# Split weights kept in device memory, and another slot schedule, in a fused four-layer float32 kernel

## The reference

```python
x = field_step(x)                                        # layer 0: stencils, once, at the start
# layer 1, for each of the 16 batch entries (S = D = 512, 16 heads of 32, F = 2048)
x = ln(src) * (1 + scale) + shift
q, k, v = x @ Wq + bq, x @ Wk + bk, x @ Wv + bv
probs = softmax(where(mask, -inf, q @ k.T / sqrt(32) + attention_bias))
x = x + (probs @ v) @ Wo + bo
h = ln(x) * g2 + beta2
x = x + gelu2(h @ W1 + b1) @ W2 + b2                     # gelu2(t) = t * sigmoid(1.702 t)
# layer 2
hidden = gelu(x @ down_W.T + down_b)                     # 512 -> 128
hidden = hidden @ expert_W[id].T + expert_b[id] + emb[id]
x = ln(hidden @ up_W.T + up_b + x) * gamma + beta
# layer 3: rotate each pair of columns
out[0::4], out[1::4] = x0*ct + x1*st, -x0*st + x1*ct     # and the same for pairs 2, 3 with phi
```

## Time and profile before

| what | value |
|---|---|
| median of three runs | 4944.82 us (4941.17 to 4945.67) |
| profiled execution, its own time | 4945.61 us |
| its span, first to last instruction | 4943.8 us |
| PE busy | 4197.9 us, 85% |
| DVE, ACT, POOL busy | 59%, 49%, 31% |
| mean granted PE clock | 0.935 of full speed |
| moved by DMA | 700.26 MB, 142 GB/s on average |

### The profile page before, as it was taken

How to read it: one execution, slowest core, us unless ns; L and a number is a source line. 1 busy time by engine, 2 the same in 40 slices (tenths; PEclk the granted TensorE clock), 3 DMA queues, 4 the chain that set the end, 5 groups by cost and what they waited for, 6 DMA issues and landing times.

```text
span 4943.8 us, 72563 instructions
## 1 busy us (share of the span) xinstructions
PE 4197.9 (85%) x25315; PEld 3075.7 (62%) x25720; DVE 2912.8 (59%) x6296; ACT 2416.5 (49%) x5064; POOL 1550.6 (31%) x1069
## 2 busy tenths in 40 slices
PE   6994789797988979797988979797978889797977
PEld 3442567575766757575766657575756667575755
DVE  8993455565555555565556555555656555555454
ACT  0002555455555555554555555455555555555542
POOL 0002124233333333233333333333333333333334
PEclk9997899899999989899999989899999989899988
DMA  3224555554545455554545455554545455554521
GB/s 118 103 95 143 168 156 163 143 153 128 162 138 164 132 154 154 143 160 125 163 133 170 135 150 152 147 165 125 161 133 164 135 148 152 151 163 126 146 88 58
DMA packets 530343, 700.26 MB, mean 142 GB/s; under 512 B 45232, under 2 KB 250848, under 8 KB 529984
## 3 DMA queue, kind: packets, MB, share of 16 engines
q1 hardware_dynamic: 521024, 677.76, 47.4%
q10 hardware_dynamic: 8448, 16.78, 0.9%
q0 software_dynamic: 512, 1.05, 0.1%
HBM read 527.20 MB, written 33.62 MB: 113 GB/s over the span
## 4 chain that ended last, share of the span: by engine, by line
PE 58%; DVE 12%; POOL 5%; ACT 4%; issue 4%; another core or an unknown queue 4%; DMA 4%; SPq 1%; POOLq 0%; ACTq 0%; DVEq 0%
PE bank L824 42%; PE bank L886 6%; PE bank L877 4%; PE bank L907 3%; DVE prob L1065 3%; POOL w L616 2%; PE bank L878 2%; POOL tok L658 1%; POOL tok L660 1%; DMA raw<-in_L_cond_W 1%; DVE zT L1114 1%; ACT probT L707 1%; DVE stats L511 1%; DMA stack<-parts 1%
## 5 line engine op out<-in xcount | busy, mean ns | idle before, releaser
L616 POOL TENSOR_TENSOR w<-raw,w 128x512 fp32r<-128x512 f32 x768 | 1031.8, 1348 | 2362.6 <-ACT w L691 2361.4
L707 ACT ACTIVATE probT<-bank 128x512 f32<-128x512 f32 x1024 | 609.8, 595 | 1569.4 <-PE bank L886 1565.5
L886 PE MATMUL bank<-ident,prob 128*128 128x128 f32 x4096 | 646.1, 282 | 303.6 <-ACT probT L707 281.7
L824 PE MATMUL bank<-zT,w 128*128 128x512 f32 x3072 | 828.1, 420 | 29.0 <-issue 28.1
L824 PE MATMUL bank<-w,gparts 128*128 128x512 f32 x3072 | 791.7, 406 | 13.2 <-DVE gparts L1120 13.2
L886 PEld LDWEIGHTS bank<-ident,prob 128*128 128x128 f32 x4096 | 520.7, 146 | 450.9 <-ACT prob L699 288.3
L699 ACT ACTIVATE prob<-prob,low 128x512 f32<-128x512 f32 x1024 | 732.5, 715 | 7.2 <-DVE low L1065 7.0
L824 PEld LDWEIGHTS bank<-zT,w 128*128 128x128 f32 x3072 | 597.1, 196 | 166.3 <-issue 36.9
L1065 DVE CUSTOM_DVE_ANT_0 prob<-bank,prob 128x512 f32<-128x512 f32 x1024 | 697.8, 681 | 0.3 <-issue 0.3
L824 PEld LDWEIGHTS bank<-w,gparts 128*128 128x128 f32 x3072 | 578.7, 189 | 133.8 <-POOL w L616 11.1
L877 PE MATMUL bank<-stack 128*128 128x512 f32 x1024 | 517.7, 506 | 165.7 <-DVE low L1065 148.3
(11 more groups left out here) (175 smaller groups left out, 5197.6 us busy)
## 6 DMA issues: line engine op xcount, KB each, us to landing
prob<-in_fside_Bx16xSxS SPq DMA_DIRECT2D x512, 512.0 KB, 3.8
stack<-parts SPq DMA_DIRECT2D x1024, 128.0 KB, 3.1
raw<-in_L_cond_W SPq DMA_DIRECT2D x512, 256.0 KB, 2.7
field<-in_x SPq DMA_DIRECT2D x16, 1024.0 KB, 5.4
x<-total ACTq DMA_DIRECT2D x16, 1024.0 KB, 5.9
xin<-x SPq DMA_DIRECT2D x16, 1024.0 KB, 6.8
raw<-in_L_cond_Wq SPq DMA_DIRECT2D x64, 256.0 KB, 3.0
raw<-in_L_cond_Wk SPq DMA_DIRECT2D x64, 256.0 KB, 4.4
```

What stands on the lines that cost most here:

```text
L616: pool.tensor_tensor(w[m % RING][:, 1, :], raw[m % RAWS][:], w[m % RING][:, 0, :].bitcast(F32), ALU.subtract).then_inc(w_lo, 1)
L707: act.activation(probT[:, m % TURNED, :], turned[:], ACT.Copy).then_inc(turn_copied, 1)
L824: mm = te.matmul(dst, stat(hs, k), mov(hm, k), start=start and n == 0, stop=stop and n == count - 1)
L886: mm = te.transpose(turned[:, k * P:(k + 1) * P], prob[:, m % PROBS, k * P:(k + 1) * P], ident[:])
```

## The change

**Weights are split once.** Only the 48 units of batch entry 0 (`FRESH`) go through `raw`, ACT and POOL. SP then stores both halves, 512 KB, to a scratch tensor `split_w` (`store_split`), and every later use is one 512 KB load from there straight into the ring (`load_split`): SP waits until PE has released the buffer and issues the load; PE waits for `w_in`. `SPLIT_AT` allows at most one fresh unit in a slot.

**ACT's order in a slot** is now `copy_turned(t)` and then `exp(t + 2)`.

**The slots move.** Feed forward, Y, layers 2 and 3, Q, K and V come 1 to 6 slots earlier. The turn of the next input goes from slot 49, where all four column blocks were turned through the `sums` banks, to slots 36 to 39, one block a slot through the bank `turned`, with the high part on ACT ahead of `copy_turned`, the rest on DVE behind its feed-forward work, and PE waiting for the latter before `turn_block`. Up and V blocks alternate in slots 50 to 56 (`UP_AT`, `UP_BANK`, `V_BANK`). `scale_context` comes one slot earlier.

**Work changes engine.** `number_mask` goes to POOL. The sine products of the rotation go to POOL (four 128 x 512 `tensor_scalar`, behind beta), and DVE is left with two `scalar_tensor_tensor` over 1024 elements. The copy into `fence` in `score_step` is gone.

```diff
-QK_AT = ((51, 52), (0, 1), (14, 15), (31, 33))
-CTX_SCALE_AT, CTX_LAST_AT, O_AT = 2, 3, 5
-Z_TURN_AT = 10
-FF_AT = 13
-STATS_AT, ADAPT_AT, LOAD_X_AT, EXPERT_AT = 18, 26, 11, 20
-Y_AT, X_TURN_AT, Y_TURN_AT = 47, 49, 51
-DOWN_AT, EXPERT_MM_AT, UP_AT = 53, 54, 55
-V_AT = (53, 54, 57, 58)
-NORM_AT, ROTATE_AT = 57, 63
-MASK_AT = (59, 60, 61, 62)
-CTX_AT = 60
-V_BANK = (1, 2, 0, 1)
+QK_AT = ((45, 47), (0, 2), (16, 18), (30, 32))
+CTX_LAST_AT, O_AT, Z_TURN_AT = 1, 3, 8
+FF1_AT, FF2_AT = 11, 14
+LOAD_X_AT, STATS_AT, ADAPT_AT, EXPERT_AT, X_TURN_AT = 8, 18, 26, 20, 36
+Y_AT, Y_TURN_AT, DOWN_AT, EXPERT_MM_AT = 44, 46, 48, 50
+V_AT, UP_AT = (50, 52, 54, 56), (51, 51, 53, 53)
+V_BANK, UP_BANK = (1, 2, 3, 2), (3, 0, 1, 0)
+NORM_AT, ROTATE_AT = 55, 62
+MASK_AT = (49, 53, 57, 61)
+CTX_AT = 57
 def ff1_slot(f):
-    return FF_AT if f == 0 else FF_AT + 2 + 2 * f - 1
+    return FF1_AT + 2 * f
 def ff2_slot(f):
-    return FF_AT + 2 + 2 * f + 2 if f < NF - 1 else Y_AT
+    return FF2_AT + 2 * f
...
+                def store_split(slot):
+                    for m in FRESH:
+                        if SPLIT_AT[m] == slot:
+                            i = ORDER[m]
+                            sp.wait_ge(w_lo, i + 1)
+                            sp.dma_start(split_w[i], w[m % RING][:].rearrange("p h n -> p (h n)").bitcast(F32)).then_inc(w_stored[m % RING], 16)
+                            if i + RAWS < len(FRESH):
+                                load_raw(sp, FRESH[i + RAWS])
+                def load_split(slot):
+                    for m in range(RING, len(UNITS)):
+                        if UNITS[m - RING][2] == slot and m not in ORDER:
+                            await_release(sp, m - RING)
+                            kind, _, k = UNITS[m][0]
+                            i = KINDS[kind, k]
+                            sp.wait_ge(w_stored[FRESH[i] % RING], 16 * same_place(FRESH[i], True))
+                            sp.dma_start(w[m % RING][:].rearrange("p h n -> p (h n)").bitcast(F32), split_w[i]).then_inc(w_in[m % RING], 16)
...
+                        if c < B and X_TURN_AT <= s < X_TURN_AT + KB:
+                            x_hi_part(c, s - X_TURN_AT)
+                        if t < BLOCKS:
+                            copy_turned(t)
                         if t + EXP_LEAD < BLOCKS:
                             exp(t + EXP_LEAD)
-                        if t < BLOCKS:
-                            copy_turned(t)
...
                 def unit(kind, b, k):
                     m = UNIT[kind, b, k]
-                    te.wait_ge(w_lo, m + 1)
+                    if m in ORDER:
+                        te.wait_ge(w_lo, ORDER[m] + 1)
+                    else:
+                        te.wait_ge(w_in[m % RING], 16 * same_place(m, False))
                     return w[m % RING]
...
                         if t < BLOCKS:
+                            if c < B and X_TURN_AT <= s < X_TURN_AT + KB:
+                                te.wait_ge(x_lo, KB * c + s - X_TURN_AT + 1)
                             turn_block(t)
...
-                    v.tensor_copy(fence[:, m % 7:m % 7 + 1], scal[:, 0, 0:1])
...
+                                for h in range(2):
+                                    sine = scal[:, a, 4 + 2 * h:5 + 2 * h]
+                                    pool.tensor_scalar(crossed[:, :, 2 * h], quads[:, :, 2 * h + 1], sine, None, ALU.mult).then_inc(sined, 1)
+                                    pool.tensor_scalar(crossed[:, :, 2 * h + 1], quads[:, :, 2 * h], sine, -1.0, ALU.mult, ALU.mult).then_inc(sined, 1)
```

More of the change, by code:

```diff
@@ L86, in weight_units, with split_slots, same_place @@
             t = SLOTS * n + s
[L87 to L88 removed]
+            if n and s == O_AT:
+                units += [(("o", n - 1, k), t, t + TB - 1) for k in range(KB)]
             for f in range(NF if n else 0):
                 if s == ff1_slot(f):
[L91 removed]
+                    units.append((("w1", n - 1, f), t, t))
                 if s == ff2_slot(f):
[L93 removed]
+                    units.append((("w2", n - 1, f), t, t))
             for g in range(1, G) if n < B else ():
                 if s in QK_AT[g]:
[L96 removed]
+                    units.append((("qk"[QK_AT[g].index(s)], n, g), t, t))
             if n + 1 < B:
                 if s in QK_AT[0]:
[L99 to L101 removed]
+                    units.append((("qk"[QK_AT[0].index(s)], n + 1, 0), t, t))
+                if s == V_AT[0]:
+                    units += [(("v", n + 1, k), t, SLOTS * n + V_AT[-1]) for k in range(KB)]
     return units
 UNITS = weight_units()
[L106 to L111 removed]
+UNIT = {name: m for m, (name, _, _) in enumerate(UNITS)}
+FRESH = [m for m, (name, _, _) in enumerate(UNITS) if name[1] == 0]
+ORDER = {m: i for i, m in enumerate(FRESH)}
+KINDS = {(kind, k): i for i, (kind, _, k) in enumerate(UNITS[m][0] for m in FRESH)}
+def split_slots():
+    slots = {}
+    last = -3
+    for m in FRESH:
+        if m >= RING:
+            last = max(last, UNITS[m - RING][2]) + 1
+            assert last < UNITS[m][1] + 2, (UNITS[m], last)
+        slots[m] = last
+    return slots
+SPLIT_AT = split_slots()
+def same_place(m, fresh):
+    return sum(1 for u in range(m % RING, m + 1, RING) if (u in ORDER) == fresh)
 class Link:
@@ L535, in early_statistics @@
         def early_statistics(link, v):
-            for q in range(TB):
-                number_mask(v, 0, q)
             v.wait_ge(x_in, 16)
@@ L574, in _ @@
                     load_bias(sp, pair)
-                next_units(-3)
-                next_units(-1)
+                store_split(-3)
                 for j in range(HG):
                     load_stack(0, j)
+                for slot in (-2, -1):
+                    store_split(slot)
+                    load_split(slot)
                 for n in range(B + 1):
@@ L627, in _ @@
                 split_lo(-3)
-                split_lo(-1)
+                for q in range(TB):
+                    number_mask(pool, 0, q)
                 pool.wait_ge(consts_in, 16 * 12)
@@ L631, in _ @@
                 pool.tensor_tensor(xin[0][:], xin[0][:], bcast(row["bo"]), ALU.add).then_inc(xin_biased, 1)
-                split_lo(0)
+                for slot in (-2, -1):
+                    split_lo(slot)
                 for n in range(B + 1):
@@ L748, in _ @@
                     q_hi(0, 0, c)
-                split_hi(-1)
                 for q in range(TB):
@@ L753, in _ @@
                     exp(m)
-                split_hi(0)
+                for slot in (-2, -1):
+                    split_hi(slot)
                 for n in range(B + 1):
@@ L801, in _ @@
                         if c < B:
-                            if s == X_TURN_AT:
-                                for k in range(KB):
-                                    x_hi_part(c, k)
                             if s in QK_AT[0]:
@@ L980, in _ @@
                                 for k in (2 * (s - Z_TURN_AT), 2 * (s - Z_TURN_AT) + 1):
-                                    turn(tok, k, z_turned)
+                                    turn(sums[k], tok, k, z_turned)
                             for f in range(NF):
@@ L1224, in _ @@
                             tail(a, s)
-                        if c < B and s in MASK_AT:
-                            number_mask(v, c, s - MASK_AT[0])
                         if n < B and CTX_AT < s < CTX_AT + G:
```

205 lines of the change are left out of this document (99 added, 106 removed).

## The result

Four runs of the changed kernel have a median of 4900.24 us (4880.8 to 4902.56), four of the kernel before 4945.24 us (4941.17 to 4950.87). The ratio is 0.990, with a 95% interval of 0.9872 to 0.9927. So the change gains 45 us, where 235 were forecast, and the time is above the range (4590 to 4860). The profiled execution took 4898.9 us, with a span of 4897.1.

What follows compares the result with a forecast made beforehand. PE bounds slots 14 to 45; elsewhere it waits for splits, mask and DVE. A middle n: 8.1 - 5.7 - 21.0 + 2.5 = -16.1 us; all n 235, so 4945.6 becomes 4711 us, range 4590 to 4860.

Steps and rivals of the forecast that it cites:

- 10.3 us wait: Old slots 60 and 61: PE waits for `copy_turned` behind weight split and DVE mask; forecast to have no cause left.
- 4.8 and 1.9 us waits: Old slots 10 to 13: waits for a weight split and for DVE's `z_lo`; forecast gone, window gain 5.7 us.
- this is covered: Feed forward: exponential delays `tanh` and `g_hi` by 0.91 us each, against about 1.3 us to spare.
- the starving feed forward: What would make the forecast most wrong: ACT's new order starves the feed forward, and all 16 column blocks pay.
- Four O loads in slot 56: 2 MB ahead of bias and stack loads, with a clock drop after the `ctx_lo` wait: may take 2.5 us per entry.
- n = 0 and n = 1: a gain of 6 and of 5: First two entries: n = 0 gains 6 us (mask, fewer splits), n = 1 gains 5 despite 512 KB stores beside 36 splits.
- hidden, unless POOL needs over 1.7: Four sine products on POOL at 1.2 us each, done 14 us after the normed rows; DVE needs them some 16 after.
- The 2 us for `g_lo` behind POOL: Slot 39: POOL's addition to xin (4.5 us) starts there and holds DVE's `g_lo`, another 2 us.
- B: Rival: DMA becomes the bound in the feed forward, a middle n gets 14 us longer, 5100 us; chance 0.07.
- A: Rival: POOL's gamma, beta and slow sine products hold `ctx_lo` and rotation, PE waits some 10 us; 4828 us; chance 0.15.
- C: Rival: PE's clock stays up without the long waits, 8 us more gained per middle n, 4607 us; chance 0.12.
- D: Rival: no help; the long wait is really the chain through beta, something as long replaces it; about 4940 us; chance 0.03.

Runs made afterwards that it cites:

- e6: Changed kernel with exponential first, `scale_context` one slot later, output bias added in slot 52, O loads spread over slots 61, 62, 63 and 0: 4720.09 us, 0.9566.
- e13: e6 with the rotation's second half done in slot 63, not directly behind the first in slot 62: 4685.69 us, 0.9477.
- e4: Changed kernel with ACT doing `exp(t + 2)` ahead of `copy_turned(t)` again, as before the change: 4835.56 us, 0.9786.
- e9: Kernel before, with only ACT's new order (`copy_turned` ahead of the exponential): 4980.51 us, 1.0074.
- e1: Changed kernel with each O unit reload cut to 64 KB of its 512 KB, leaving out part of the computation: 4837.27 us, 0.9776.
- e10: Changed kernel with the four O loads in full, issued one each in slots 61, 62, 63 and 0, not together in slot 56: 4839.14 us, 0.9795.
- e11: Changed kernel with every one of the 720 stored-weight reloads cut to 64 KB, stores unchanged, leaving out part of the computation: 4816.43 us, 0.9743.
- e2: Changed kernel with `scale_context` back by one slot, from slots 17, 33 and 49 to 18, 34 and 50: 4854.59 us, 0.9816.
- e12: e11 with the stores of split blocks cut to 64 KB too: 4804.64 us, 0.972.
- e7: Changed kernel with exponential first, `scale_context` one slot later, output bias added in slot 52, gamma and beta in quarters; O loads still in slot 56: 4799.17 us, 0.9717.
- e14: e13 with a second operation (times 1.0) in the two sine products that had one: 4665.81 us, 0.9418.
- e8: e6 with gamma and beta in quarters and a second operation (times 1.0) in the plain sine products: 4710.02 us, 0.9521.

## Why the prediction was wrong

Per entry, by its own stretches (e6 is the changed kernel with four delays taken out, e13 with five):

| slots | predicted | changed kernel | e6 | e13 |
|---|---|---|---|---|
| 3 to 11 | 36.3 | 36.2 | 35.0 | 35.3 |
| 12 to 42 | 143.8 | 149.7 | 143.3 | 142.8 |
| 43 to 2 | 80.4 | 86.3 | 81.3 | 78.0 |
| all | 260.5 | 272.2 | 259.6 | 256.2 |

The main mechanism was right: with the splits gone the 10.3 us wait of the earlier trace rows and the 4.8 and 1.9 us waits of the earlier trace rows are gone, and the longest wait of PE in n = 2 to 14 is 5.1 us. That slots 3 to 11 came out to 0.1 us is in part luck: the terms given for them add up to 36.1, not 36.3, and 1.1 us of what was measured is the delay of `z_hi` in slot 11 that no term held (e4). The likeliest case was priced for a schedule without collisions, and four of its steps failed.

- *"this is covered"* (the exponential ahead of `tanh` and `g_hi`). It holds in the plain slots. It fails where the block's `g_hi` meets POOL's addition in slot 39, and outside the feed forward, for `z_hi` in slot 11 and in slots 44 and 50, which the step didn't look at. The sum put it at nothing. Measured 5.4 us per entry (e4), 65 us, 4.2 of them together with POOL's addition; in the kernel before the same edit costs 40 us (e9). The prediction named the starving feed forward as what would make it most wrong; it was a few slots, not all sixteen blocks.
- *Four O loads in slot 56: "2.5"*, for queue and clock together. The trace of before had no 2 MB ahead of small loads. Measured 5.4 and 5.6 us in slots 61 to 63 (e1, e10), 63 and 61 us in all. The price per byte wasn't the error: 214 MB more took 600 us more of the engines (60.1% of 4897.1 less 47.4% of 4943.8), 0.73 us for 256 KB where 0.91 was reckoned, and e11 shows that the rest of the traffic costs 0.7 us per entry by the traces, and by the medians 23 us in all at most. The forecast named the small loads behind the 2 MB; what it had too low is how long they and PE wait there.
- *The move of `scale_context`*, from slot 2 to slot 1 of sixteen, is in no line of the sum. It put DVE's wait for `pv` ahead of `g_lo`: 3.4 us per entry (e2).
- *n = 0 and n = 1: a gain of 6 and of 5.* They lost 6.2 and 12.5 us, 30 in all against the forecast. The stores were named there but given no price; they cost 12.3 (e11, e12). What the other 6 us over the kernel before are, and why the 11 us of gain didn't come, stays open.

Taken out together, the delays of the first three steps give 12.5 us per entry (e6), where the forecast was off by 11.7 and had 2.5 and 2 in its sum for two of them. e6 meets the forecast of slots 12 to 42 partly by luck: the 143.8 us hold 2 for POOL's addition, which e6 no longer has there.

Smaller: the rotation was put at 2.2 us in slot 62; taking it apart gave 3.3 in slot 0, the clock included (e13). The sine products were taken as 1.2 us each, "hidden, unless POOL needs over 1.7"; they take 2.0 on average, 8.1 us for four, so the bound was passed, yet DVE waited for them in only two of sixteen rotations. For gamma and beta ahead of `ctx_lo` 2.8 us stood in the sum, and slot 60 lost 3.2 (e7). The 2 us for `g_lo` behind POOL were 4.2.

The sum: thirteen entries missed 11.5 us each, 149 us; n = 0 and 1, 30; n = 15 and 16, 11, less 1 at the start. That is, but for rounding, the 188 us between 4711 and the profiled 4898.9.

Of the rivals, B fell: DMA was at 0.64 in slots 12 to 42 of n = 6, where the forecast said near 0.75, and the list of waits has none of PE for a load of `w`. Loads did cost time, but in slots 61 to 63, and with all bytes moved that time was gone (e10). A is right in what it says of POOL (slow products, and DVE's `ctx_lo` held for 3.91 us beside beta), but e7 shows that removing it gave nothing while the loads were late. C didn't come: the mean clock is 0.943. D fell: nothing as long took the place of the 10.3 us wait, and e6, which only takes back or moves parts of the change, runs 220 us below the kernel before (e14, with a further edit to the rotation, 281). No run has the stored weights without the moved slots, so how the gain divides between the two is not shown.

## What to carry to other kernels

When a change reissues large loads in place of small ones, read which small load stands behind them in the same queue and when it is due; spreading them over four slots gave 61 us here. When instructions change places in an in-order engine's program, follow the delayed one to the next engine and see whether it now falls on the other side of a lock: 0.7 us became 4.7. Cost every step that a diff moves, by a single slot too: 1.7 us, twice in each of thirteen entries, is 44 us.

## What was unexpected of the hardware

A strided 128x512 TENSOR_SCALAR on POOL takes 2.86 us with one operation and 1.20 us with two (medians of 32), on tiles of the same shape; adding a multiplication by 1.0 took the first to 1.18 us (e8). The Trainium skill calls GpSimd's one-input operations roughly line rate (*GPSIMD Engine Reference*, section 4.1), from which the prediction made an estimate of 0.5 us. The measurements differ from it, and decide. Why the second operation helps, no run here shows.
